# The same kernel with its on-chip buffers moved from odd multiples of 32 bytes to multiples of 64 bytes

## What is computed

```python
x = x + xattn(layernorm(x), ctx_1024, ...)   # 256 queries, 25088 context rows, width 512
x = x + attn(layernorm(x), ...)              # 16 heads of 64, half-causal mask
x = x + ffn(layernorm(x), ...)               # shared SwiGLU + top-1 of 32 experts, 512 x 1024 x 512
```

## The kernel before

| buffers | before | after |
|---|---|---|
| `ident`, `ones`, `upper`, `iota32` | multiples of 64 | the same addresses |
| `x`, `cols`, `st` | 19136, 23232, 23360, multiples of 64 | 64 higher |
| `small` with `acc`, `pt_hi`, `q_hi`, `q_lo`, `s2c`, `y`, two tile homes, `xg`, `hh`, `dd`, `scat`, ... | 24352 and on, odd multiples of 32 (remainder 32 by 256) | 24448 and on, remainder 128 by 256 |
| `logits`, `onehot`, `tok` and their neighbours | multiples of 64 already | 128 higher (`tok` 192) |
| all at `RINGB` | 81888 and on, odd multiples of 32 (remainder 224 by 256) | 81856 and on, remainder 192 by 256 |

## Time and profile before

### The profile page before, as it was taken

One profiled execution on the slowest core, in us unless ns is written; L12 is line 12 of the kernel. 1 busy time (PEld: TensorE's weight loads), 2 busy tenths in 40 slices (PEclk: granted clock), 3 DMA queues, 4 the chain that ended last, 5 costly groups with the idle time before them and its releaser, 6 DMA issues.

```text
span 1173.9 us, 16777 instructions
## 1 busy us (share of the span) xinstructions
PE 1048.5 (89%) x6736; PEld 712.8 (61%) x6736; DVE 618.7 (53%) x977; ACT 373.1 (32%) x546; POOL 3.5 (0%) x20
## 2 busy tenths in 40 slices
PE   9999999999999999999999999999976666666666
PEld 8867888878888888888775846444432222222223
DVE  4457888878878878878764265322121111111112
ACT  2444456456446546546533253000000000000000
POOL 1000000000000000000000000000000000000000
PEclk9999999999999999999999999999998989989988
DMA  9548899887788878778749344999999999999997
GB/s 347 184 144 307 306 338 334 301 311 262 275 298 273 284 275 296 281 267 307 269 168 406 120 186 184 427 427 425 427 427 426 428 428 425 428 429 428 428 427 296
DMA packets 91122, 381.48 MB, mean 325 GB/s; under 512 B 5584, under 2 KB 6224, under 8 KB 74064
## 3 DMA queue, kind: packets, MB, share of 16 engines
q1 hardware_dynamic: 91088, 381.00, 84.1%
HBM read 355.29 MB, written 25.69 MB: 325 GB/s over the span
## 4 chain that ended last, share of the span: by engine, by line
DMA 45%; PE 33%; DVE 16%; SPq 3%; ACT 2%; issue 2%; DVEq 0%; ACTq 0%
DMA deep<-in_r_down 23%; DMA strips<-turned 10%; DMA pt<-strips 8%; DVE nat_lo L1258 4%; PE ps L981 4%; DVE pt_lo L1263 3%; DVE turned L1285 3%; DMA wide<-in_r_up 3%; SPq L348 3%; DVE st L1270 2%; PE ps L541 2%; ACT pt_hi L1049 2%; PE ps L556 2%; PE ps L557 2%; PE ps L555 2%
## 5 line engine op out<-in xcount | busy, mean ns | idle before, releaser
L555 PE MATMUL ps<-ctt_hi,q_hi 128*128 128x512 f32 x392 | 155.8, 397 | 0.0
L557 PE MATMUL ps<-ctt_hi,q_lo 128*128 128x512 f32 x392 | 154.6, 394 | 0.0
L556 PE MATMUL ps<-ctt_lo,q_hi 128*128 128x512 f32 x392 | 154.6, 394 | 0.0
L570 PE MATMUL ps<-nat_hi,pt_lo 128*128 128x512 f32 x368 | 145.6, 396 | 0.0
L568 PE MATMUL ps<-nat_hi,pt_hi 128*128 128x512 f32 x368 | 145.2, 394 | 0.1
L569 PE MATMUL ps<-nat_lo,pt_hi 128*128 128x512 f32 x368 | 145.1, 394 | 0.0
L1202 ACT ACTIVATE sg<-ps 128x256 f32<-128x256 f32 x32 | 12.3, 384 | 390.2 <-PE ps L961 390.2
L1599 DVE TENSOR_TENSOR hh<-sg,ps 128x256 f32<-128x256 f32 x32 | 13.5, 421 | 231.1 <-PE ps L967 231.1
L981 PE MATMUL ps<-deep,hh_t 128*32 128x512 f32 x496 | 75.9, 738 | 54.1 <-DMA deep<-in_r_down 54.1
L1253 DVE TENSOR_TENSOR ctt_lo<-ctt,ctt_hi 128x2048 fp32r<-128x2048 f32 x49 | 111.0, 2289 | 21.7 <-ACT ctt_hi L1041 21.6
L1045 ACT ACTIVATE nat_hi<-nat 128x2048 fp32r<-128x2048 f32 x48 | 92.0, 1916 | 82.4 <-DMA nat<-in_ctx_rows 82.4
(11 more groups left out here) (281 smaller groups left out, 1254.7 us busy)
## 6 DMA issues: line engine op xcount, KB each, us to landing
wide<-in_r_gate SPq DMA_DIRECT2D x32, 2048.0 KB, 26.0
wide<-in_r_up SPq DMA_DIRECT2D x32, 2048.0 KB, 27.4
deep<-in_r_down SPq DMA_DIRECT2D x31, 2048.0 KB, 25.9
ctt<-in_ctx_t SPq DMA_DIRECT2D x49, 1024.0 KB, 8.0
nat<-in_ctx_rows SPq DMA_DIRECT2D x48, 1024.0 KB, 7.3
strips<-turned SPq DMA_DIRECT2D x96, 256.0 KB, 5.7
pt<-strips SPq DMA_DIRECT2D x24, 1024.0 KB, 4.8
w_gate<-in_w_g_t SPq DMA_DIRECT2D x2, 1024.0 KB, 14.2
```

What stands on the lines that cost most here:

```text
L555: mm(o, qh, ctt_hi[par][:, c, :], start=(c == 0), stop=False)
L556: mm(o, qh, ctt_lo[par][:, c, :], start=False, stop=False)
L557: last = mm(o, ql, ctt_hi[par][:, c, :], start=False, stop=(c == HC - 1))
L570: last = mm(o, p_lo[:, w, :], n_hi[:, t, :], start=False, stop=(final and t == KT - 1))
```

## The change

The rounding of sizes in `place` goes from 32 to 64 bytes, and the base of the upper region goes down by 32 bytes to a multiple of 64. Every buffer's offset then is a multiple of 64. No instruction, wait, DMA, size or order is changed; operands keep their shapes.

```diff
         LOW = 16512
-        RINGB = 81888
+        RINGB = 81856
         WB = D * FI * 4 // P
@@
             t = at(name, shape, dt, cursor[0])
-            cursor[0] += (size + 31) // 32 * 32
+            cursor[0] += (size + 63) // 64 * 64
             assert cursor[0] <= RINGB, (name, cursor[0])
```

## The result

The changed kernel takes 1168.8 us (1166.5 to 1170.7 over 5 runs) against 1176.7 beside it. The ratio is 0.9937, with a 95% interval of 0.9920 to 0.9953. "No change" was forecast with 0.78. The profiled execution has a span of 1166.3 us, 7.6 less than before.

The account below looks back on a forecast made before the run. TensorE, with the device-memory round trip close behind, was taken to bound the context loop, and the DMA rate stage 3. Zero for VectorE, ScalarE, TensorE and DMA on 1173.9 us, plus 3.3 us around it, gave 1177.2; range 1170 to 1182.

Parts of the forecast that it names:

- No change: Whole kernel: no effect beyond what measurement can tell, about 0.3% or 3.5 us; chance 0.78.
- What bounds the kernel: Context loop: TensorE at 22.4 us a pair, device-memory round trip at most 0.7 us shorter; stage 3: DMA at 427 GB/s.
- The round trip: Context loop: chain storing to and loading from device memory, 22.3 us a pair, claimed as second bound beside TensorE.
- VectorE, ScalarE, DMA into SBUF: Loop instructions and stage 3 weight loads: each taken as zero; the loads' bounds were 5.7 us faster, 5.0 us slower.
- DMA out of SBUF: Loop stores of `turned`: at most 0.9 us off a 5.84 us store, worth zero because TensorE's loop is longer.
- TensorE: All 2352 fp32r matmuls: taken as zero, bounds -2.5 to +2.5 ns each, 5.9 us either way.
- 20 ns per matmul with no owner: Each fp32r matmul: 233.3 ns against 213.3 at the column rate; the most a better address could return.
- Rival 1: Fp32r matmuls: TensorE streams faster from multiples of 64; 5.9 us to 1171, or 8 us to 1169; chance 0.08.
- What would show it: Numbers to stay: 48 weight loads per 11.20 us, VectorE 1222 ns, `pt_hi` 1052 ns, 427 GB/s, store near 5.8 us.

Follow-up runs that it names:

- e4: Kernel before the change with only the upper region's base moved, 81888 to 81696, so all large buffers have remainder 32 by 256; 1164.8 us, ratio 0.9896.
- The bench: Separate kernels without the layer: matmul groups, 1 MB stores and loads at chosen remainders by 256 bytes; fp32r matmuls of 512 columns took 226.7 to 234.2 ns.
- e5: Changed kernel with the lower large buffers at remainder 64 by 256 instead of 128, all still at multiples of 64; 1175.5 us, ratio 0.9993 against the kernel before.
- e3: Changed kernel with the upper region's base at 81792 instead of 81856, all large buffers at remainder 128 by 256; 1163.6 us, ratio 0.9882 against the kernel before.

## Why the prediction missed

**What bounds the kernel** was read rightly: TensorE in the loop and the DMA rate in stage 3. The round trip was weighed too heavily in "whatever speeds up one alone brings little": e4 made TensorE's pair 0.64 us shorter, just inside the 0.7 that the prediction left it, and the middle of the loop followed without a gap. The round trip took its share of the gain only in a few single waits near both ends of the loop.

**VectorE, ScalarE, DMA into SBUF**: taken as zero, and they were. 1222 and 1052 ns are unchanged, the rate of stage 3 is 428 GB/s against 427.

**DMA out of SBUF**: a small effect of the place exists, 0.05 to 0.09 us a lone store, and it was rightly called covered. The rule of the Trainium skill that the prediction quoted ("DMA: Bandwidth & Descriptors", section "How a descriptor splits into AXI transactions") gives the right sign from 224 to 192 but not the order: by an estimate from its figures a piece at remainder 32 would pay one beat more than an aligned one and a piece at 224 seven. The bench has these two alike (6.14 and 6.13 to 6.17 us), while 128, four beats by the same estimate, is faster than both (5.95). The measurement decides.

**TensorE** is the term that failed. The step was "I take zero": zero with an end at -2.5 ns a matmul, taken from fp32 matmuls; it measured -4.4, 233.3 to 228.9. The fp32 rows could not show it: the bench has 429.2 ns for them at every distance. The text said that these rows do not settle fp32r, and then still took its value and its range from them. The other row, 20 ns per matmul with no owner, was the right one to widen the range by. It was dismissed because the figure was the same beside busy and idle engines. That shows only that no other engine causes it; that TensorE's two operands could stand well or badly to each other was left out. The range's lower end had a slip besides: 1177.2 less the 8.2 of its own bounds is 1169.0, not 1170. The measured 1168.8 lies a little below that too.

**Rival 1** came close with its price, 8 us to 1169 against 7.9 to 1168.8, but by luck. The 8 us were half of the round trip's slack, 0.35 us a pair; what happened was 0.43 us a pair (22.40 to 21.97) less the single waits. Its mechanism was wrong. It held that multiples of 64 are read faster; e4 has no large buffer at one and is faster still, e5 has all and gains nothing measurable. Its cap of 17 us, to 1160 from 7 ns on, was not put to the test, since no placement saves more than 6.6 ns.

**What would show it** worked: the first number to watch, 11.20 us for 48 weight loads, moved, and TensorE waited on `pt_lo`, as rival 1 said. VectorE, ScalarE and stage 3 stood. The store, which was to stay near 5.8 us, went from 5.7 to 5.3; this follows the loop and not the place, as above.

**What stays open.** That reads of the two operands meet in the memory is a guess: bf16 and fp32 matmuls have two operands as well and are free of the effect, and no run looks into the memory. Why 64 is nearly as good as 0 but 192 is not, and why 256 columns reverse the sign, is not explained. Nor is it settled what `pt_lo`, at distance 0 all along, does to the products, and whether the place of the next matmul's weights counts beside that of the matmul's own. And e3 and e4, both at distance 0, differ by 1.2 us at their medians, which is within their spread.

## What to carry to other kernels

For fp32r matmuls of 512 columns whose weights are reloaded every time, give the moving and the stationary operand the same remainder by 256 bytes, at a multiple of 32; look at start distances, not at busy time, to see whether it took. A row from another data type is no bound for an operation that goes through its columns nearly twice as fast (226.7 to 234.2 ns against 429.2), and a cost without an owner belongs in the range. When a second path is within a few percent of the bound, look where it really holds the bound up, here in a few pairs and not in each, and before moving a load back, read how long its reader already waits.

## What the runs showed of the hardware

- An fp32r matmul of 512 columns at a granted clock of 1.00 takes 226.7 to 227.5 ns with its two operands at distance 0 by 256 bytes, 229 at 64, 232.2 to 232.4 at 128 and 233.1 to 234.2 at the other multiples of 32.
- With both operands at remainder 8 it takes 11.12 us for 48, 231.6 ns, although the distance is 0.
- In bf16 (215.8 ns) and fp32 (429.2 ns a record) no distance matters. The page "TensorE: Matmul & The Clock Gate" of the Trainium skill (section "Wait — 56ns, not 53.3ns?") has 215.7 ns for a matmul of 512 columns at the full clock, and the bench agrees for bf16; fp32r at the best placement found, 226.7, is 10.9 ns above the bench's bf16.
- A store of 1 MB from SBUF in pieces of 2048 bytes takes 5.89 us from a multiple of 256, 5.95 from remainder 128, 6.08 from 64 or 192 and 6.12 to 6.17 from odd multiples of 32.
